# Where an attention mask is turned: a transposing DMA in place of TensorE, and a normalisation moved to GpSimd

## What is computed

```python
h = maximum(layernorm(x), 0)                       # over the 256 features
Wh = einsum('bnf,fo->bno', h, W)
f1 = Wh @ a[:256]; f2 = Wh @ a[256:]
e = f1[:, :, None] + f2[:, None, :]
e = where(e >= 0, e, 0.2 * e)
attention = softmax(where(adj > 0, e, -9e15), axis=1)   # over i, for each j
out = x + elu(einsum('bij,bjo->bio', attention, Wh))
```

## Time and profile before

| | us |
|---|---|
| median of 3 runs | 989.98 (989.9 to 990.5) |
| the profiled execution | 988.09 |
| its span, first to last instruction | 986.3 |
| PE busy | 949.7 (96%) |
| DVE busy | 925.5 (94%) |
| ACT busy | 919.9 (93%) |
| POOL busy | 543.5 (55%) |
| granted TensorE clock, mean | 0.995 |

### The profile page before, as it was taken

How to read it: one execution, slowest core, us unless ns; L and a number is a source line. 1 busy time by engine, 2 the same in 40 slices (tenths; PEclk the granted TensorE clock), 3 DMA queues, 4 the chain that set the end, 5 groups by cost and what they waited for, 6 DMA issues and landing times.

```text
span 986.3 us, 23846 instructions
## 1 busy us (share of the span) xinstructions
PE 949.7 (96%) x8988; PEld 836.8 (85%) x8988; DVE 925.5 (94%) x1269; ACT 919.9 (93%) x1345; POOL 543.5 (55%) x566
## 2 busy tenths in 40 slices
PE   8878999999999999999999999999999999999996
PEld 5666988889889888888888898888988888898785
DVE  7799999999899999999989999999999999999975
ACT  3799999999999999999999999999999999988985
POOL 5556544565556665665655655556554655465440
PEclk9899999999999999999999999999999999999999
DMA  9577667799869889799979988879986987979635
GB/s 222 89 107 104 97 116 121 139 159 167 152 123 179 153 152 166 121 174 158 164 143 142 171 152 155 152 138 165 166 152 121 175 142 133 154 124 150 120 76 171
DMA packets 199092, 142.13 MB, mean 144 GB/s; under 512 B 7361, under 2 KB 187841, under 8 KB 198978
## 3 DMA queue, kind: packets, MB, share of 16 engines
q0 software_dynamic: 140160, 81.80, 61.6%
q1 hardware_dynamic: 58818, 58.81, 19.9%
HBM read 176.16 MB, written 16.84 MB: 196 GB/s over the span
## 4 chain that ended last, share of the span: by engine, by line
PE 39%; ACT 22%; issue 20%; DVE 8%; POOL 7%; DMA 3%; SPq 0%; ACTq 0%; DVEq 0%; POOLq 0%
ACT prob L581 8%; PE pre L408 5%; PE tp L430 5%; PE acc_st L477 5%; PE acc L495 5%; PE acc L502 5%; PE acc_st L478 5%; PE acc L497 5%; PE acc_st L479 5%; POOL direct L892 3%; ACT stored L595 3%; ACT prob L589 2%; DVE stored L788 2%; DVE direct L783 2%; ACT part L617 1%
## 5 line engine op out<-in xcount | busy, mean ns | idle before, releaser
L769 DVE CUSTOM_DVE_ANT_0 prob<-tp,f_row 128x2048 f32<-128x2048 bf16 x128 | 292.1, 2282 | 16.5 <-DMA f_row<-f_scratch 11.3
L477 PE MATMUL acc_st<-v,stored 128*128 128x256 f16 x960 | 261.5, 272 | 0.6 <-ACT part L617 0.6
L479 PE MATMUL acc_st<-v,stored 128*128 128x256 f16 x960 | 261.6, 273 | 0.0
L478 PE MATMUL acc_st<-v,stored 128*128 128x256 f16 x960 | 261.6, 273 | 0.0
L589 ACT ACTIVATE prob<-prob,shift 128x2048 f32<-128x2048 f32 x128 | 256.5, 2004 | 3.9
L581 ACT ACTIVATE prob<-prob,f 128x2049 f32<-128x2049 f32 x128 | 257.8, 2014 | 2.3 <-DVE prob L769 1.9
L892 POOL TENSOR_TENSOR direct<-prob,inv 128x1024 f16<-128x1024 f32 x128 | 243.2, 1900 | 10.0
L886 POOL TENSOR_SCALAR small_total<-total 128x1 f32<-128x1 f32 x128 | 28.9, 226 | 378.0 <-ACT prob L589 378.0
L495 PE MATMUL acc<-v,direct 128*128 128x256 f16 x1024 | 231.9, 273 | 3.8 <-ACT z_direct L623 3.3
L497 PE MATMUL acc<-v,direct 128*128 128x256 f16 x1024 | 231.8, 273 | 0.0
L783 DVE SCALAR_TENSOR_TENSOR direct<-prob,inv,direct 128x1024 f16<-128x1024 f32 x128 | 162.1, 1267 | 9.5 <-POOL direct L892 9.5
(11 more groups left out here) (93 smaller groups left out, 1351.4 us busy)
## 6 DMA issues: line engine op xcount, KB each, us to landing
raw<-in_adj POOLq DMA_DIRECT2D x64, 1024.0 KB, 10.3
y<-in_x SPq DMA_DIRECT2D x63, 256.0 KB, 2.9
out<-y SPq DMA_DIRECT2D x63, 256.0 KB, 2.2
y<-elu POOLq DMA_DIRECT2D x56, 256.0 KB, 4.5
x_in<-in_x SPq DMA_DIRECT2D x108, 128.0 KB, 3.8
f_row<-f_scratch SPq DMA_DIRECT2D x31, 256.0 KB, 6.6
stored<-in_x SPq DMA_DIRECT2D x4, 512.0 KB, 6.1
f_scratch<-f_t SPq DMA_DIRECT2D x124, 0.5 KB
```

The lines of the kernel that those rows point to most:

```text
L477: nc.tensor.matmul(bank[:, 0:FO], p_st[:, 0, rows], v_c[:, 0, :], start=(c == 0), stop=False)
L478: nc.tensor.matmul(bank[:, 0:FO], p_st[:, 0, rows], v_c[:, 1, :], start=False, stop=False)
L479: last = nc.tensor.matmul(bank[:, 0:FO], p_st[:, 1, rows], v_c[:, 0, :], start=False, stop=(c == G - 1))
L769: nc.vector.tensor_tensor_reduce(out=prob[:, c % 2, 0:N], in0=tp_b, in1=f1_row[:, b % 2, :], scale=1.0, scalar=-3.0e38, op0=ALU.add, op1=A ...
```

## The change

- **Mask.** GpSimd now issues `cast_adj`: a DMA from `adj` in DRAM to a bf16 copy in DRAM (`adj_bf16`), all 2048 rows of 2 chunks' columns at a time for the first batch and of 4 chunks' columns for the others, 36 in all, 8 to 12 steps ahead of use. SP issues `turn_adj`: one transposing DMA for each chunk, of 2048 rows by 128 columns of the copy, to 128 partitions by 2048 in SBUF (`mask`, 6 buffers), 5 steps ahead. `make_mask` works in place on that buffer, in SBUF. `mask_scores` reads it there: both of its inputs are now in SBUF. The 16 transposes of a chunk on PE, `neg`, `raw` and the bf16 identity go.
- **Normalise.** For chunks 19 and up `normalise` leaves ACT and runs on GpSimd, right behind `split_high` in a step.
- **Head.** The first group of four chunks is split for the root and the offset, so that chunk 0 has its own; the order of some small DVE operations changes, PE does 5 more warm-up transposes, ACT loads its table and scales W earlier, and `make_mask(0)` and `make_mask(1)` come two steps later.
- **End.** In batch 6 the elu pieces are finished up to three steps sooner (`ORDER_NEXT_TO_LAST`).

The core of the diff. `turn_adj` is SP's, `transpose_mask` PE's, the removed `normalise` ACT's, `make_mask` and `mask_scores` DVE's, the rest GpSimd's.

```diff
+    RM = 6
+    adj_dram = nc.dram_tensor("adj_bf16", [B, N, N], BF16, kind="Internal").ap()
-        raw = sb("raw", [P, 2, C, 2 * P], BF16)
-        neg = sb("neg", [P, 2, C, P], BF16)
+        mask = sb("mask", [P, RM, N], BF16)
...
+        ORDER_NEXT_TO_LAST = {2: [4], 3: [0], 5: [1], 6: [5], 7: [2], 9: [3], 10: [6], 12: [7]}
...
+        def root_group(i):
+            return (range(0, 1), range(1, 4))[i] if i < 2 else range(4 * i - 4, 4 * i)
...
+        def slab_chunks(i):
+            return range(2 * i, 2 * i + 2) if i < C // 2 else range(4 * i - C, 4 * i - C + 4)
+        def slab_at(s):
+            early = {-16: 0, -12: 1, -8: 2, -4: 3}
+            if s in early:
+                return [early[s]]
+            return [i for i in range(4, SLABS) if slab_chunks(i).start - (8 if i < C // 2 else 12) == s]
+        def turned_at(s):
+            if s < 0:
+                n = {-8: (0, 1), -4: (2, 3), -1: (4,)}.get(s, ())
+            else:
+                n = (s + 5,) if s + 5 < CH else ()
+            return n
...
+            def turn_adj(n):
+                c = n
+                slab = slab_of(c)
+                sp.wait_ge(adj_cast[slab % 4], 16 * (slab // 4 + 1))
+                wait(sp, scores, c + 1 - RM)
+                b, j = divmod(c, C)
+                sp.dma_start_transpose(mask[:, c % RM:c % RM + 1, :], adj_dram[b][:, j * P:(j + 1) * P]
+                                       ).then_inc(mask_in[n % RM], 16)
...
-            def transpose_mask(c):
-                pe.wait_ge(neg_ready, c + 1)
-                wait(pe, scores, c)
-                for m in range(C):
-                    last = nc.tensor.transpose(tp_b[:, m * P:(m + 1) * P], neg[:, c % 2, m, :], ident_b[:])
-                last.then_inc(tp_ready, 1)
...
-            def normalise(c):
-                nc.scalar.activation(xn_buf(c), x_buf(c), ACT.Identity, scale=rstd[:, c % RS:c % RS + 1],
-                                     bias=offset[:, c % RS:c % RS + 1]).then_inc(xn_ready, 1)
...
             def make_mask(c):
-                dve.wait_ge(raw_in[pair % 2], 16 * (pair // 2 + 1))
-                wait(dve, tp_ready, c - 1)
-                nc.vector.tensor_scalar(neg[:, c % 2], raw[:, pair % 2, :, c % 2 * P:(c % 2 + 1) * P], 0.0, -NOT_AN_EDGE, ALU.is_le, ALU.mult
+                dve.wait_ge(mask_in[c % RM], 16 * (c // RM + 1))
+                m = mask[:, c % RM, :]
+                nc.vector.tensor_scalar(m, m, 0.0, -NOT_AN_EDGE, ALU.is_le, ALU.mult).then_inc(neg_ready, 1)
...
             def mask_scores(c):
-                dve.wait_ge(tp_ready, c + 1)
+                dve.wait_ge(neg_ready, c + 1)
...
-                    out=prob[:, c % 2, 0:N], in0=tp_b, in1=f1_row[:, b % 2, :], scale=1.0, scalar=-3.0e38,
+                    out=prob[:, c % 2, 0:N], in0=mask[:, c % RM, :], in1=f1_row[:, b % 2, :], scale=1.0, scalar=-3.0e38,
...
-            def load_raw(pair):  
-                wait(pool, neg_ready, 2 * pair - 2)
-                nc.gpsimd.dma_start(raw[:, pair % 2], adj[b].rearrange("(c p) j -> p c j", p=P)[
-                    :, :, 2 * P * q:2 * P * (q + 1)]).then_inc(raw_in[pair % 2], 16)
+            def cast_adj(i):
+                wait(pool, adj_cast[i % 4], 16 * (i // 4))
+                chunks = slab_chunks(i)
+                cols = slice(j * P, (j + len(chunks)) * P)
+                nc.gpsimd.dma_start(adj_dram[b][:, cols], adj[b][:, cols]).then_inc(adj_cast[i % 4], 16)
...
             for s in range(FIRST, END + 2):
                 if chunk(s - 1):
                     split_high(s - 1)
+                if chunk(s + LEAD + 2) and s >= 0:
+                    normalise(s + LEAD + 2)
```

More of the change, by code:

```diff
@@ L382, in _ @@
                     load_x(s + 24)
+                for n in turned_at(s):
+                    turn_adj(n)
                 if chunk(s + LEAD - 1) and (s + LEAD - 1) % 4 == 3 and read_alone((s + LEAD - 1) // 4):
@@ L818, in _ @@
                     mask_scores(s)
+                if offset_at(s) is not None and s < 0:
+                    make_offset(offset_at(s))
                 for c in measured_at(s):
```

120 lines of the change are left out of this document (59 added, 61 removed).

## The result

The median is **1240.5 us** (1235.4 to 1246.9), against 989.9 before: a ratio of 1.253, with a 95% interval of 1.250 to 1.256. The profiled execution took 1235.4, its span 1233.6. The forecast was 1220, slower. The direction and the main mechanism came out as forecast. That the sum came out within 20 us is in part luck: one term was too large, two were far too small, and they nearly cancel. Executions of one kernel here can differ by some per cent, and medians and ratios take those within 1.5% of its fastest.

What follows compares the result with a forecast made beforehand. PE was taken to bound the kernel before; afterwards DVE and GpSimd excluding each other gives 9.0 us a step: 127 steps make 1143, with head, tail and small terms 1220 us. The range was 1090 to 1520 us.

Steps and rivals of the forecast that it cites:

- The bound before: Kernel before: PE sets the pace, 7.15 of 7.20 us a step, with ACT at 6.99 and DVE at 6.94 right behind.
- The exclusion: With both `mask_scores` inputs in SBUF, GpSimd's long operations cannot run beside it; step of 8.0 to 9.9 us, chance 0.67.
- the case at 1270: By the skill page's port rule, GpSimd's `root` adds its full time every fourth step, about 0.4 us a step; near 1270 us.
- The sum of a step: DVE and GpSimd path in one step: 2.21 + 3.27 + 2.38 + 0.47 + 0.60 + 0.07, together 9.0 us.
- `normalise`, 0.60: `normalise` on GpSimd right behind `direct`, where DVE's L783 wants to start, adds 0.60 us a step.
- 8.4 a step where `normalise` costs nothing: Case where `normalise` falls under the v part and costs nothing: 8.4 us a step, 1143 us in all.
- The signs: Expected in the trace: stretched `small_total` and `inv`, `direct` not beside `mask_scores`, PE and ACT about 70%, DVE over 95%.
- The DMAs: Cast 3.3 and transposing DMA 3.5 us a step with the rest make 8.6, just below DVE's 9.0; bounds 5.8 to 13.1.
- the rival that was given 0.18: DMAs set the pace from 9.0 us a step on, `make_mask` waits for its mask; 1470 us, chance 0.18.
- SP's queue: SP's f1 reads, residual load and output store stand behind `turn_adj` but wait for later events anyway; cost nothing.
- The head: Start of the kernel: a cast and a transposing DMA behind each other in place of one load cost 1 us.
- PE's clock: PE's 2.9 us of idle time a step could lower its clock, making 6.1 us a step 12.2; nothing was taken.

Runs made afterwards that it cites:

- e8: Kernel after, with `mask_scores` reading a zero constant in PSUM and the casts of batches 1 to 7 left out; 995.8 us.
- e1: Kernel before, with `mask_scores` taking its mask from `neg` in SBUF instead of PSUM, all else kept; 1156.3 us, 1.168 times before.
- e2: Kernel after, with `mask_scores` reading a zero constant in PSUM; casts, transposing DMAs and `make_mask` stay; 1212.6 us.
- e5: Kernel after, without the casts of batches 1 to 7; all transposing DMAs read the first batch's copy; 1176.8 us.
- e4: Kernel after, with SP issuing the last read of the f1 row ahead of the transposing DMA; 1217.3 us.
- e11: Kernel after, with each 2 MB cast in four DMAs of 512 rows, one a step, and f1 read ahead of the transposing DMA; 1195.4 us.
- e12: Kernel after, with casts in quarters, f1 read first, and `mask_scores` reading a zero constant in PSUM; 1190.1 us.
- e9: Kernel after, with casts from batch 2 on in slabs of 512 whole rows, issued 12 steps sooner; 1272.6 us at best.

## Why the prediction was right, and where it wasn't

**The bound before** was read rightly. "No change on PE alone can bring more than about 0.2 us a step" agrees with e8, where the transposes are gone and neither the exclusion nor most casts are there: 7.06 us in a usual step against 7.13.

**The exclusion** is shown. e1 has it alone and gives 1156 us; in the traces of e1 and of the kernel after, `small_total` ends with `mask_scores` in 119 and 107 of 128 steps (7 before), and `direct` meets `mask_scores` in 2 and in 1 (118 before), and then the later of the two is the one that is stretched. The reading that it takes two SBUF inputs rests on the one edit of e1 and on its mirror, e2. The Trainium skill, "SBUF — State Buffer", section "SBUF: two separate sides", has one pair of ports for the two engines, held for a whole instruction: for the long operations and for `small_total` and `inv` the traces agree. Its consequence for `root`, the case at 1270, is not what the trace shows: one `root` began at 523.53, `mask_scores` started 0.29 us behind it and took its usual 2.28, and it was `root` that took 3.46 us. No DVE instruction beside a `root` of the kernel after is longer than usual.

**The sum of a step** was 9.0 and measured 8.54. Term by term in the step shown above: start to start of the next DVE instruction 606.27 - 604.05 = 2.22 (said 2.21); from there to L804 3.26 (3.27, taken from one stall in the kernel before); L804 and L809 1.20 and 1.34 (1.19 each); elu 0.60 in this step (0.47 as a mean over all steps); `normalise` nothing of its own. **The term that failed is `normalise`, 0.60.** "Right behind `direct`, where DVE's L783 wants to start": it does start there, at 609.48 against 609.53, but DVE's work was done first. L804 kept its 1.28 and `normalise` was stretched to 1.60; L809 took 1.42 in place of 1.28. So it cost DVE 0.14 us, and this happens in about half of the steps: over all of them L809 takes 1350 ns in the mean, against 1280 in e1, which has `normalise` on ACT. The forecast's own last sentence had this case: 8.4 a step where `normalise` costs nothing. With 0.07 in place of 0.60 the sum is 8.47, with 0.14 it is 8.54. That the exclusion has one price for an engine that is asked first and another for one that comes second was in the earlier trace rows already, where `inv` was the one that was stretched.

**The signs.** `small_total` and `inv` were stretched and `direct` left `mask_scores`, as was said. PE and ACT are at 77% and 74% in the long stretch, near the 70% that were said. "DVE busy over 95% with waits inside" did not come: DVE is at 76% there. Its waits stand mostly ahead of its instructions, for ACT's v, `direct`, x and f1, and the hidden ones are on GpSimd.

**The DMAs** were 8.6 in the forecast, "just below DVE's 9.0". Both prices were near: 3.3 was said for the cast and 3.9 came out, 3.5 for the transposing DMA and 3.3 came out, with the other traffic beside them. The Trainium skill, "DMA: Bandwidth & Descriptors", section "Latency and other measured facts", has 261 GB/s for the latter; here it was 512 KB in 3.3 us, 159 GB/s (181 by e5's 2.9 us), and the value taken between the two bounds from q1's rows was the better guide. But the order of the two limits came out less clear than that: the mean step is 8.80 us with the DMAs and no exclusion (e2), 8.52 with the exclusion and hardly a cast (e5), and 8.98 with both. So the rival that was given 0.18 is in part true beside the forecast. It didn't show as it was said to, by `make_mask` waiting for its mask: the masks have five steps of slack and the row of f1 and x have less. The right forecast would have been to ask which transfer has the least slack.

**SP's queue**: "these wait for later events anyway: nothing". This step failed. It counted the waits of the transposing DMA and not the time that its issue holds the queue, 3.3 us in the median and 12.5 at most, while casts were in flight (2.2 in the median in e5, without them). No row of the kernel before shows such an issue, and it should have been bounded, not set to nothing. The boundaries cost 57 us more than before, and e5 shows that they don't without the casts. e4 puts 17 of the 57 on the order of one read. How much of the rest is the queue and how much the slow transfers isn't told apart.

**The head** was to cost 1 us, "where a cast and a transposing DMA stand behind each other". It cost 21. The casts of 1 MB and the transposing DMAs were under way together there, with a DMA share of 1.34 and 1.21, and the issue of the first two transposing DMAs held SP's queue for 16.4 us, with f1's way through DRAM behind it. The first mask was 12.0 us late, the second another 7.3, the row of f1 another 4.3.

**PE's clock**: nothing was taken, and nothing shows against it in a usual step. It was granted 0.50, the lower of its two levels (1.2 GHz), from 40 to 60 us, when PE had nearly nothing to do, 0.95 in the long stretch of the kernel after and 0.99 in e5's. In the 20 us at 0.50 PE was busy for 0.66. But PE did not fall to 6.1 us a step: without the transposes' 136.1 us it was busy for 949.7 - 136.1 = 813.6 us before and for 922.1 after. How much of these 108 us is clock and how much is waiting inside instructions isn't told apart; PE didn't set the pace of the step shown above.

So 1220 against 1240 is (9.0 - 8.54) x 120 = 55 us too much for the usual steps, and 7 x (16.55 - 9.0) = 53 at the boundaries, 20 in the head and 3 from the profiled execution to the median too little. Errors of 55 and 76 that have nothing to do with each other left 20: that part of the agreement is luck.

**What stays open.** That something on the side of the DMAs holds a step near 8.8 us without the exclusion is shown by e2 and e8, which differ in the casts alone. What it consists of, the rate of the 16 engines or SP's queue, isn't: e11 moved its (125.9 + 81.8) / 128 = 1.62 MB a step in some 8.75 us a step in most batches, and e12, with more freedom, was hardly quicker; and a share above 1 says that packets of several queues stand in an engine at once, so the share can't be read as work. The transposing DMAs on a queue of their own, with nothing behind them, weren't tried. A kernel with the mask turned by DMA and read from PSUM wasn't tried. No version run here beats the kernel before.

## What to carry to other kernels

Before an operand moves from PSUM to SBUF, look at what runs on GpSimd while that instruction is in DVE: in this kernel, with two SBUF inputs, neither of the two large instructions became longer in the usual step, but they no longer ran together, and what was hidden is added to the step, here 1.4 us of 7.1. Look for it in short GpSimd instructions that are suddenly six times as long. Where two limits lie close, removing either alone brings little (28 or 64 us of 245), so remove both in one experiment before judging either. And when work goes to DMAs, count for each queue how long an issue holds it, and look first at the transfer with the least slack, not at the new one.

## What the runs showed of the hardware

- The issue of a transposing DMA of 2048 rows by 128 bf16 columns held SP's queue for 1.6 to 12.5 us, 3.3 in the median, where a plain DMA issued by itself held it for 0.3 to 1.5, 0.5 in the median; with denser casts up to 25.1 (e9).
- It cost 3.3 us of all 16 DMA engines for 512 KB, as much as q1 had taken for more than two steps of its other work; 2.9 with hardly a cast beside it (e5) and 3.8 with the casts spread out (e11).
- A cast from DRAM to DRAM took 105 ns a packet of 2 KB read and 1 KB written, against 69 for the loads before with half of each, and 2 MB landed after 20.0 us.
- Where `mask_scores` with two SBUF inputs and GpSimd's `direct` met, once in the kernel after and twice in e1, the later one waited: `direct` took 3.47 us in place of 1.9 when it came second, and `mask_scores` 3.67 in place of 2.28 when it did (e1). With one input in PSUM they ran together in 118 of 128 steps of the kernel before, and neither was longer.
- When GpSimd's `normalise` began 0.05 us ahead of a two-input DVE operation, in 65 steps of the kernel after, DVE's kept its duration, GpSimd's took 1.60 us instead of 0.6, and the DVE operation behind took 1.42 instead of 1.28.
- GpSimd's `root`, of 4 elements a partition, never held up DVE, not even when it had begun 0.29 us earlier; it was the one that took 3.46 us.
